# An expert layer on one core: the products of the experts' outputs moved from the head of a step to between its two scatter halves

## What is computed

```python
q = (xn @ w_q.T).reshape(b, n, 2, h, kd).transpose(2, 0, 1, 3, 4)   # xn: x after batch norm
sim = jnp.einsum('pbnhd,hkpd->pbnhk', q, keys)
s, i = jax.lax.top_k(sim, k)
...
scores, pk = jax.lax.top_k(all_scores, k)
idx = jnp.take_along_axis(all_idx, pk, axis=-1)
w_down = key_in[idx]
w_up = key_out[idx]
o = jnp.einsum('bnd,bnhkd->bnhk', inputs, w_down)
o = jax.nn.gelu(o, approximate=False) * jax.nn.softmax(scores, axis=-1)
return jnp.einsum('bnhk,bnhkd->bnd', o, w_up)
```

## Time and profile before

| | us |
|---|---|
| median of 3 runs | 565.7 (564.43 to 568.42) |
| the profiled execution | 564.61, its span 562.8 |
| TensorE busy with matmuls | 370.1 (66% of the span) |
| VectorE busy | 447.9 (80%) |
| ScalarE busy | 242.6 (43%) |
| GpSimd busy | 230.3 (41%) |
| mean granted clock of TensorE | 0.725 of full speed |

### The profile page before, as it was taken

How to read it: one execution, slowest core, us unless ns; L and a number is a source line. 1 busy time by engine, 2 the same in 40 slices (tenths; PEclk the granted TensorE clock), 3 DMA queues, 4 the chain that set the end, 5 groups by cost and what they waited for, 6 DMA issues and landing times.

```text
span 562.8 us, 24195 instructions
## 1 busy us (share of the span) xinstructions
PE 370.1 (66%) x10097; PEld 285.2 (51%) x10097; DVE 447.9 (80%) x2767; ACT 242.6 (43%) x377; POOL 230.3 (41%) x311
## 2 busy tenths in 40 slices
PE   5686775175469566865777485738674876586554
PEld 3233563035266556564646463737464655565554
DVE  2538896999996799789979995899799979984441
ACT  3867613453335235533555344433542545252221
POOL 1034400452952265435675461447263717250400
PEclk9889865776659575967696578666965787577758
DMA  8700000000000000000000000000000000000000
GB/s 233 144 0 2 0 1 0 1 1 5 2 6 1 5 2 23 1 5 2 24 2 3 23 3 3 3 21 5 3 4 23 3 4 2 23 2 5 2 22 20
DMA packets 7644, 8.94 MB, mean 16 GB/s; under 512 B 880, under 2 KB 6896, under 8 KB 7408
## 3 DMA queue, kind: packets, MB, share of 16 engines
q1 hardware_dynamic: 6960, 7.34, 4.9%
q10 hardware_dynamic: 576, 0.07, 0.1%
HBM read 5.31 MB, written 2.10 MB: 13 GB/s over the span
## 4 chain that ended last, share of the span: by engine, by line
PE 48%; DVE 25%; issue 14%; ACT 11%; DMA 1%; SPq 0%; ACTq 0%; POOL 0%; DVEq 0%
PE psum L826 15%; PE psum L803 14%; PE psum L813 10%; PE psum L722 4%; DVE arena L642 4%; PE psum L783 3%; DVE idx L587 3%; ACT arena L411 2%; DVE arena L499 2%; DVE arena L645 2%; ACT nat L431 2%; DVE arena L646 2%; DVE arena L639 2%; DVE x L549 1%; DVE picked L611 1%
## 5 line engine op out<-in xcount | busy, mean ns | idle before, releaser
L803 PE MATMUL psum<-arena 64*64 64x16 f16 x8192 | 115.5, 193 | 125.7 <-issue 61.1
L803 PEld LDWEIGHTS psum<-arena 64*64 64x64 f16 x8192 | 108.7, 142 | 140.5 <-issue 104.2
L826 PE MATMUL psum<-ko,arena 64*128 64x128 f32 x1024 | 92.7, 357 | 3.7 <-issue 3.7
L826 PEld LDWEIGHTS psum<-ko,arena 64*128 64x128 f32 x1024 | 88.9, 269 | 5.0 <-issue 4.6
L411 ACT ACTIVATE arena<-psum 128x1024 f32<-128x1024 f32 x32 | 32.6, 1019 | 127.0 <-PE psum L803 127.0
L587 DVE FIND_INDEX8 idx<-vals,sims 128x8 uint32<-128x32 f32 x512 | 82.7, 185 | 0.0
L282 POOL TENSOR_TENSOR arena<-arena 128x512 f32<-128x512 f32 x60 | 74.4, 1275 | 8.3 <-ACT arena L411 8.3
L642 DVE TENSOR_TENSOR arena<-iota,listsT 128x4096 f16<-128x4096 f16 x32 | 75.5, 2360 | 0.0
L235 POOL TENSOR_TENSOR cand<-vals 128x128 f32<-128x128 f32 x16 | 11.4, 710 | 150.8 <-DVE vals L579 150.8
L813 PE MATMUL psum<-x1T,trn 128*64 128x256 f32 x512 | 59.3, 385 | 7.0 <-ACT arena L417 7.0
L579 DVE MAX8 vals<-sims 128x8 f32<-128x32 f32 x512 | 49.2, 175 | 14.8 <-ACT sims L377 14.7
(11 more groups left out here) (106 smaller groups left out, 580.6 us busy)
## 6 DMA issues: line engine op xcount, KB each, us to landing
x<-in_L_attn_x_dram SPq DMA_DIRECT2D x8, 256.0 KB, 5.4
out_dram<-nat SPq DMA_DIRECT2D x8, 256.0 KB, 2.1
ko<-in_L_ffn_key_out_dram SPq DMA_DIRECT2D x2, 512.0 KB, 10.3
nat<-in_L_ffn_key_in_dram SPq DMA_DIRECT2D x2, 256.0 KB, 8.7
nat<-in_L_ffn_keys_dram SPq DMA_DIRECT2D x2, 128.0 KB, 5.6
nat<-in_L_attn_W_delta_dram SPq DMA_DIRECT2D x1, 64.0 KB, 2.8
nat<-in_L_attn_W_in_dram SPq DMA_DIRECT2D x1, 64.0 KB, 2.7
nat<-in_L_attn_W_select_dram SPq DMA_DIRECT2D x1, 64.0 KB, 2.7
```

Of the source, the lines that this page charges most:

```text
L803: end = pe.matmul(psum[64 * e:64 * e + 64, at:at + NJ], hotx[rows, g, :, e], hotw[rows, part, g, :, e], start=(part == 0), stop=(part == 1))
L826: end = pe.matmul(y2[:, e, m % 2], gl[rows, m % 4, j, :], ko[rows, j, :], start=(j == 0), stop=(j == NJ - 1))
```

## The change

The call of `experts_out(m-3)` moves, within the step, from ahead of `lists_turned` to between the two scatter halves. The wait ahead of it changes from `lists_evac` at m-1 to `lists_evac` at m. The two calls after the loop stay as they are.

```diff
             scores(0)
             scores(1)
             for m in range(NS + 1):
-                if m >= 3:
-                    wait(pe, "lists_evac", m - 1)
-                    experts_out(m - 3)
                 if m >= 1:
                     lists_turned(m - 1)
                 if 2 <= m + 1 < NS:
@@ -841,6 +838,10 @@
                     experts_in(m // 2)
                 if m >= 1:
                     scatter(m - 1, 0)
+                if m >= 3:
+                    wait(pe, "lists_evac", m)
+                    experts_out(m - 3)
+                if m >= 1:
                     scatter(m - 1, 1)
             wait(pe, "lists_evac", NS)
             experts_out(NS - 2)
```

## The result

The changed kernel takes 657.6 us (median of 4 runs, 654.08 to 660.14), the kernel before 566.2 in the same comparison (564.43 to 568.42): 1.161 times as long, 95% interval 1.153 to 1.168. The prediction was 640 us, between 622 and 658: the sign and the mechanism as forecast, the size at the very edge, 0.4 us inside the range and with two of the four runs outside it. The profiled execution took 654.08 us, with a span of 652.3; the one before had 562.8. So 89.5 us of span are to be placed.

What follows compares the result with a forecast made beforehand. No engine alone was taken to bound the kernel, but how TensorE and VectorE hand work to each other. 564.6 + 81.2 (even steps) - 6.4 (odd steps) = 639.4 us, as a median 640, range 622 to 658.

Steps and rivals of the forecast that it cites:

- The wait: Even steps: `residual` waits for the moved product behind the first scatter half, some 11 us in each of seven steps.
- The even step's size: Growth of each even step: 5.2 scatter half, 6.2 product, 0.2 start offset; 11.6 us, seven times +81.2, bounds 8.4 to 13.1.
- The odd steps: Seven odd steps, m = 3 to 15: together -6.4 us, a middle one +0.2, bounds -20 to +20.
- Turning the lists: Odd steps: lists turned 3.7 us after the scatter's end, no longer after a product of 6.5 us: -2.8 us.
- a slow scores group: Odd steps: after a 3.7 us pause TensorE's clock is low, so turning and scores cost +1.5 us.
- The product between the halves: Odd steps: the product costs 5.5 us, less 1.1 us of waiting for the copy that it covers: +4.4 us.
- The second half: Odd steps: the second scatter half follows a product, not a pause, and goes from 6.3 to 4.7 us: -1.6.
- The next even step's lists: After odd steps: VectorE takes up the lists earlier, and the first scatter half follows: -1.3 us; behind step 15, -3.7.
- The filled pause: Rival: the product covers TensorE's 29.8 us of waiting for the copy and nothing gets late: 536 us, chance 0.01.
- The case in which TensorE keeps its upper level: Rival: TensorE stays at 2.4 GHz through scatter, product, scatter: 604 us, covering 604 to 622, chance 0.09.
- The case of no change: Rival: `residual` doesn't in fact wait for the moved product: 566 us, chance 0.01.
- The case of piled-up gaps: Rival: TensorE's low level and gaps for instructions pile up: 677 us, covering 658 to 677, chance 0.09.

Runs made afterwards that it cites:

- e5_fill: The changed kernel with three idle float32 matmuls ahead of the turning of the lists in odd steps: 658.4 us against 565.6 for the kernel before.
- e3_residual_later: The changed kernel with `residual` one step later, in the odd step, `spread2` and `norm_out` behind the copy: 589.6 us against 568.9 for the kernel before, ratio 1.038.
- e4_copy_first: The kernel before, with ScalarE's `spread2` and `norm_out` behind the copy of the first scatter half: 563.2 us against 568.9 without the edit, ratio 0.989.
- e6_shift: The changed kernel with 32 small float32 matmuls once ahead of the loop: 672.0 us against 565.6 for the kernel before.

## Why the prediction was right, and which terms were off

**The wait** was the step that decided, and it is as described: seven waits of line 651, 85.6 us without the one at the end (92.8 in all), where about 80 were expected. With the odd steps alone, where it is absent, 80 of 91 us go; with `residual` and what hangs on it moved out of its way, 71. That the time fell inside the range is in part luck: 14.7 us are missing in the sum for the profiled run (639.4 against 654.08), and the median lies 3.5 us above that run, where 1.1 was added; 0.5 us more would have been outside.

**The even step's size** was 11.6 us and is 12.3. Of its parts, the first scatter half was put at 5.2 us and took 6.0 in the mean: three of the seven have two gaps for instructions, as at 405.27, where the half takes 7.5. The product was put at 6.2 and took 6.0. The link from `residual` to the second half was right to 0.1 us. Five of the missing 14.7 us are here; 0.7 are at start and end. The upper bound of this term was read too low: after step 14 the product began at 491.86 and the lists were turned at 499.83, 8.0 us and not 7.6, which makes it 13.5 instead of 13.1.

**The odd steps** were put at -6.4 us and came to +2.6: the other nine. This was the part that failed, since a gain was forecast and none came. The sign of being wrong that the prediction names, a middle odd step that gains or loses more than 2 us, is not met by the mean (+1.6, from second half to first half of even steps) but by three of the five one by one (+4.4, -3.3, +4.6).
- Turning the lists 3.7 us after the scatter's end was right (3.77), and so was a slow scores group, if a little small: from turning to `experts_in` 3.5 to 4.1 us instead of 2.1, where 3.6 was put. Not counted in the middle steps was that `experts_in` begins slowly too: its first 16 matmuls (as the trace counts them) take up to 2.5 us instead of 1.95, and 3.7 in step 15. Together 3.6 us of the nine. The reason given, the pause, does not hold in odd steps (`e5_fill`). Nor does the row at 0.55 show it: in the kernel before, the scatter half ahead of that pause (133.9 to 139.9) was at 0.50 already.
- The product between the halves was put at 5.5 and took 6.0: twice a gap fell into it, 6.9 and 8.4 us.
- The second half came near full clock as expected (granted 0.81 to 1.00), 4.4 to 5.5 us where it has one gap and 6.2 with two, 5.1 in the mean where 4.7 was put: 2.7 us of the nine. The first half got shorter, 4.4 instead of 5.5, which was not foreseen; with the product it gives 2.6 us back.
- The next even step's lists were put 1.3 us earlier. From the end of the scatter to the next first half it is 10.6 us and not 9.9: the tables, now started earlier, fall under GpSimd's multiplications, line 639 takes 1.60 us instead of 0.7. Behind step 15 it is worst: of 3.7 us expected 0.9 came, because the first tables of step 16 took 7.0 us instead of 4.1. In sum 6.1 of the nine, the largest term.

The lists turned in odd steps are 0.7 us better than put, and 3.6 + 2.7 - 2.6 + 6.1 - 0.7 = 9.1 for the six stretches after step 4; the one with step 3 gained 0.2 more than put. With these terms the nine is placed.

**The rivals.** The filled pause (536 us) is out, and `e3_residual_later` shows that it would be out even without `residual`: the product does not fit a pause of 1 to 3 us, and the pause gives less than its length, since gaps for instructions come back where it was (`e4_copy_first`). The case in which TensorE keeps its upper level was half right: the second halves of odd steps did run at or near 1.00, but in even steps the first halves were at 0.50 to 0.60 and the second at 0.50. The case of no change (566 us) is out by the waits of line 651. The case of piled-up gaps, 658 to 677 us, names a part of the misses, and its lower end is 0.4 us away; three of the seven even steps and two of the seven odd products show it.

## What to carry to other kernels

Before a piece of work is moved into another engine's idle time, look up who waits for its result and where that waiter stands in its own queue: here the idle time was itself made by that waiter, two engines away, and the move closed a chain scatter half, product, `residual`, second tables, copy, second half that had been two parallel ones. Ask second what the idle time was good for besides waiting; in a stretch that is short of instructions it is refill time, and of some 16 us taken out of such pauses only 6 came through.

## What the runs showed of the hardware that was not expected

- TensorE, in a stream of 16-column matmuls each with its own load, stands at multiples of 128 matmuls (256 instructions) for up to 2.8 us, 61 us in the kernel before; the place moves with every instruction added ahead (152 to 88 for 64). The Trainium skill, "Runtime: NRT & Kernel Launch", section "Instruction fetch mechanics", gives blocks of 256 instructions, which agrees, and says that fetching is mostly hidden, which doesn't hold here.
- A wait of 2.7 us just ahead of a scatter half did not prevent a gap of 2.55 us after 88 of its matmuls (`e6_shift`); after waits of 9.0 us all seven second halves of even steps ran past the first such place without one. What decides when the next instructions are asked for is not shown.
- Filling of 2.9 us at a granted clock of 0.50 did not bring the clock back (`e5_fill`).
- Table instructions of VectorE and multiplications of GpSimd side by side: 8.2 against 4.1 us for the four tables of a half, 7.9 against 4.9 for the four multiplications.
